# Metaformer block on one core: another order of the two tiles in router, convolution and end, and dummy matmuls in waits

## The chip, the cores and the metric

The kernel runs on one core of a Trainium2 chip. A core has five engines with a program of their own: TensorE (PE, matrix products), VectorE (DVE), ScalarE (ACT), GpSimd (POOL) and SyncE (SP, which here sends for data). They meet through semaphores alone. The metric is the device time of one execution in microseconds, median over the runs. The profile shows for TensorE the clock that was granted: 1.00 is 2.4 GHz, 0.50 is 1.2 GHz.

## The reference

The input `x` is (8, 32, 24, 24) in float32. Four residual parts follow each other; each normalises over the 32 channels of a pixel first:

```python
x = x + neighbour_attention(_ln_c(x))        # 4 heads, 3x3 neighbours, softmax over the nine
t = _to_tokens(x)
t = t + experts(_ln_t(t))                    # 16 experts: softmax of the logits over the 576 tokens,
                                             # the 8 best tokens pooled, gelu layer of 128, result put
                                             # back to those 8 tokens with their probabilities
x = _from_tokens(t, x)
x = x + patch_attention(_ln_c(x))            # 1x1 convolution, 9x9 patches, a @ (b^T @ c) / 9
t = _to_tokens(x)
t = t + steps(_ln_t(t))                      # 33 steps, each: op = argmax(h[0, 0, :19]); attention
                                             # and/or a two-layer relu network, where a mask allows op
```

Of the 33 steps most change nothing, since their masks exclude the chosen operation. With these inputs one step runs, and it is a relu network.

## The kernel before, in words

The eight images are two tiles, t = 0 and 1, of 128 rows each (4 images x 32 channels) and 576 pixels, worked in halves of 288. All of it stays on the chip. Each engine has one program, and the order of the work on an engine is the order of the calls written there (for PE the list of lines 690 to 800); no scheduler stands behind it.

- **Normalisation i of tile t** (i = 0 to 3, ahead of each part): PE subtracts the mean (`centre` L468, or `add_centred` L527 where the terms of a sum are added up centred), ACT squares (L906), DVE keeps the centred values (L1086), PE averages (`variance` L478), ACT forms the inverse deviation (`inverse_std`, L920 and L922), PE widens it to all rows (`widen` L488), DVE multiplies (`scale` L1093, or `patches` L1104 for the convolution).
- **Attention.** Products of q and neighbours on DVE and POOL, `head_sum` L518, softmax on DVE and ACT with the sum of exponentials on PE (L717); `spread` L541 copies the weights over the channels, DVE multiplies by v (L1121), POOL and DVE sum in threes, `add_centred` adds input and sums.
- **Router.** `gate` L549 (logits), ACT adds the bias (L929), DVE `selection` finds the eight best (L1128 to L1131) and forms `pick` (L1134), ACT `probabilities` (L934). PE `turn_y` L557 and `turn_pick` L567 transpose, `pooling` L576, `replicate` L582 and L583, `hidden` L590 and L593, `expert_out` L601, `expert_turn` L608, `scatter_centred` L616 and `scatter_raw` L623 put the results back.
- **Convolution.** `pixels_out` L636, DVE writes the columns (L1177), `mab_product` L646, ACT copies U (L955), `gram_pair` L660, DVE masks (L1185), ACT copies (L961), `values_of` L670, ACT copies (L966), `turn_back` L680, DVE `residual3` adds (L1191).
- **Choice and step.** `token_of` L686 brings the first token to one row, DVE `choose` (L1199 to L1209) finds the operation and reads the number of the next step that has work from a table `code` into `ctrl`. `strike_out` (L1214, L1216) takes the steps up to that one out of the table. Every engine then runs a loop that goes on while `ctrl` names a step: SP sends for its weights (L373 to L377), PE runs L856 and L866, ACT and DVE the relus (L1067, L1366), DVE adds the result to y (L1377). POOL adds y = h + x after the last normalisation (L448), which holds if no step has work.
- **Dummies.** `keep_clock(n, bank)` L461 runs n matmuls of 288 columns whose result nobody reads. Before, it stands around the sum of exponentials alone, two and two.

Of the kernel before, what the change touches and what calls it, by code (L numbers as in the profile page):

```python
# [11 lines left out]
T = B // TB  # L12
# [10 lines left out]
R, NP = 9, 3  # L23
# [130 lines left out]
def metaformer(nc, x, L1_ffn_ffn_w1, L1_ffn_ffn_b1, L1_ffn_ffn_w2, L1_ffn_ffn_b2, L1_ffn_wq, L1_ffn_wk, L1_ffn_wv, L1_ffn_wo,  # L154
# [5 lines left out]
    with ctx:  # L160
# [173 lines left out]
        @block.sync  # L334
        def _(sp):
            for g in range(2):
                sp.dma_start(cut(x_in, 0)[:, g, :], x[0:TB].rearrange("b c h w -> (b c) (h w)")[:, g * HS:(g + 1) * HS]).then_inc(x_ld[g], 16)
            sp.dma_start(mask_w[:, :], masks).then_inc(mask_ld, 16)
            sp.dma_start(rowc[:, :], codes).then_inc(mask_ld, 16)
            sp.dma_start(qkv_bd[:, :, :].rearrange("p a b -> p (a b)"), qkv).then_inc(qkv_ld, 16)  # L340
            sp.dma_start(wpk[:, :], pack).then_inc(pack_ld, 16)
            sp.dma_start(ew1[:, :, :].rearrange("p e h -> p (e h)"), experts1).then_inc(ew1_ld, 16)
            sp.dma_start(ew2[:, :, :].rearrange("p e o -> p (e o)"), experts2).then_inc(ew2_ld, 16)
            for t in range(T):
                sp.dma_start(U[:, t, :, GW:GW + V2], values).then_inc(value_ld, 16)


            steps, cr, row_no = (sp.alloc_register(n) for n in ("sp_steps", "sp_code", "sp_row"))
            sp.reg_mov(steps, 0)
            sp.wait_ge(ctrl_rdy, 1)  # L350
            sp.reg_load(cr, ctrl[0:1, 0:1])
            with sp.While(lambda: sp.snap(cr) < NONE):
                c_ = sp.snap(cr, min_val=0, max_val=NONE - 1)
                sp.reg_mov(row_no, (c_ >> 16) * NOPS + ((c_ >> 1) & 31))
                rw = sp.snap(row_no, min_val=0, max_val=NB_ * NOPS - 1)

                def of_step(w):

                    if len(w.shape) == 4:
                        return w.rearrange("b o c d -> (b o) c d")[bass.ds(rw, 1), :, :].rearrange("o c d -> (o c) d")  # L360
                    return w.rearrange("b o c -> (b o) c")[bass.ds(rw, 1), :].rearrange("o c -> c o")

# [15 lines left out]
                sp.reg_add(steps, steps, 1)  # L378
                wait_for(sp, ctrl_rdy, sp.snap(steps, min_val=1, max_val=NB_) + 1)
                sp.reg_load(cr, ctrl[0:1, 0:1])  # L380

            done = sp.snap(steps, min_val=0, max_val=NB_)
            for t in range(T):
                wait_for(sp, fin_rdy[t], done + 1)
                sp.dma_start(out[t * TB:(t + 1) * TB].rearrange("b c h w -> (b c) (h w)"), y[:, t, :]).then_inc(out_st, 16)
            sp.wait_ge(out_st, 16 * T)
# [3 lines left out]
        def _(pool):  # L390
# [61 lines left out]
        def _(pe):  # L452
# [268 lines left out]
            spread(0)  # L721
            spread(1)
            spread(2)
# [22 lines left out]
            gate(0)  # L746
            turn_y(0)
            variance(1, 1)
            turn_pick(0)
            widen(1, 1)  # L750
            pooling(0)
            gate(1)
            replicate(0)
            turn_y(1)
# [3 lines left out]
            turn_pick(1)  # L758
            expert_out(0)
            pooling(1)  # L760
            expert_turn(0)
            replicate(1)
            scatter_centred(0)
            hidden(1)
            scatter_raw(0)
            expert_out(1)
            variance(2, 0)
            expert_turn(1)
            widen(2, 0)
            scatter_centred(1)  # L770
            scatter_raw(1)
            pixels_out(0)
            variance(2, 1)
            mab_product(0)
            widen(2, 1)
            for k in range(4):
                gram_pair(0, k)
            pixels_out(1)
# [3 lines left out]
            mab_product(1)  # L782
            values_of(0, 2)
            for k in range(4):
                gram_pair(1, k)
            turn_back(0)
            values_of(1, 0)
            pe.wait_ge(x3_rdy[0], 1)
            token_of(xs[3])
            gram_pair(1, 4)  # L790
            centre(3, 0)
            values_of(1, 1)
            variance(3, 0)
            values_of(1, 2)
# [99 lines left out]
        def _(act):  # L894
# [109 lines left out]
            logits(0)  # L1004
            probabilities(0)
            inverse_std(1, 1)
# [42 lines left out]
            with act.While(lambda: act.snap(cr) < NONE):  # L1049
# [10 lines left out]
                with act.If((c_ & 1) > 0):  # L1060
# [9 lines left out]
                    for t in range(T):  # L1070
                        wait_for(act, fin_rdy[t], act.snap(steps, min_val=0, max_val=NB_) + 2)
# [10 lines left out]
        def _(dve):  # L1082
# [42 lines left out]
            def selection(t):  # L1125
# [5 lines left out]
                nc.vector.match_replace(rest[:, t, :], top8[:, t, :], logit[:, t, :], -3e38).then_inc(rest_rdy[t], 1)  # L1131
                dve.wait_ge(rest_rdy[t], 1)
# [87 lines left out]

            keep(0, 0, 0)
# [42 lines left out]
            scale(1, 1)  # L1264
            turned_pick(0)
            pooled_images(0)
            selection(1)
# [23 lines left out]
            residual3(0, 0)  # L1291
            choose(0, 0)
            residual3(0, 1)
            residual3(0, 2)
# [17 lines left out]
            with dve.While(lambda: dve.snap(cr) < NONE):  # L1312
                strike_out(dve.snap(steps, min_val=0, max_val=NB_))
                c_ = dve.snap(cr, min_val=0, max_val=NONE - 1)
                with dve.If((c_ & 256) > 0):
# [34 lines left out]
                    for t in range(T):  # L1350
                        dve.wait_ge(fin_rdy[t], 1)
# [18 lines left out]
                with dve.If((c_ & 1) > 0):  # L1370
# [12 lines left out]
                    for t in range(T):  # L1383
                        dve.wait_ge(fin_rdy[t], 1)
# [11 lines left out]
                dve.sem_inc(step_end, 1)  # L1396
                wait_for(dve, ctrl_rdy, dve.snap(steps, min_val=1, max_val=NB_) + 1)
                dve.reg_load(cr, ctrl[0:1, 0:1])

# [26 lines left out]
```

## Time and profile before

| | |
|---|---|
| time, median of 3 runs | 155.51 us (152.48 to 155.91) |
| the profiled execution | 155.16 us, its span 153.3 us |
| mean granted clock of TensorE | 0.771 |
| busy: PE, DVE, ACT, POOL | 129.2 (84%), 68.0 (44%), 43.5 (28%), 46.7 us (30%) |

Times in the trace count from the start of the span. In the page's second section each digit is a tenth of busy time in one of 40 slices of 3.8 us, and the line PEclk is the granted clock in tenths. The chain that ended last is followed back from the last instruction: each row starts when it was released, and lasts until it released the next. A count behind a matmul row counts passes; a float32 matmul is two of them, a transposition one.

### The profile page before, as it was taken

What the parts mean: (1) busy time and instruction counts of PE and PEld (TensorE: products, weight loads), DVE (VectorE), ACT (ScalarE), POOL (GpSimd) and SP (SyncE); (2) the same over time, 40 slices, a digit from 0 to 9 for tenths busy, and PEclk for the clock granted to TensorE, in tenths of its full rate; (3) what the DMA queues carried; (4) which work ended last, traced back from release to release, by engine and by line L of the source; (5) the groups of instructions that cost most, each with busy time, mean ns of one, the idle gap of its engine ahead of it and who ended that gap; (6) DMA issues with size and microseconds to landing.
All of it is one profiled execution on the core that took longest, in us unless ns stands there. A gap on an engine that the chain in (4) does not pass through costs nothing.

```text
span 153.3 us, 2162 instructions
## 1 busy us (share of the span) xinstructions
PE 129.2 (84%) x779; PEld 86.5 (56%) x779; DVE 68.0 (44%) x148; ACT 43.5 (28%) x104; POOL 46.7 (30%) x37
## 2 busy tenths in 40 slices
PE   0998989959999996669699999999999969647980
PEld 0365548923445572656599685775985836514630
DVE  0246985477645616232410312532650542445860
ACT  3251430410000506602810052114326314132622
POOL 8994950007917899930000000000000000303000
PEclk9999999996559999655555555559999965995567
DMA  5980000000000000000000000000000000010004
GB/s 155 377 181 0 4 0 4 0 0 0 2 0 0 0 4 0 2 0 0 0 0 0 4 0 0 0 0 0 0 0 4 0 0 0 4 17 4 2 4 154
DMA packets 3394, 3.55 MB, mean 23 GB/s; under 512 B 1974, under 2 KB 2614, under 8 KB 3384
## 3 DMA queue, kind: packets, MB, share of 16 engines
q1 hardware_dynamic: 3096, 2.90, 6.3%
q10 hardware_dynamic: 288, 0.51, 0.9%
q8 instruction: 7, 0.11, 0.3%
q14 instruction: 3, 0.02, 0.1%
HBM read 2.81 MB, written 0.59 MB: 22 GB/s over the span
## 4 chain that ended last, share of the span: by engine, by line
PE 78%; DVE 8%; ACT 6%; issue 4%; DMA 2%; DVEq 1%; ACTq 0%
PE PS L527 9%; PE PS L541 7%; PE PS L494 5%; PE PS L468 5%; PE PS L488 4%; PE PS L856 4%; PE PS L660 4%; PE PS L670 4%; PE PS L636 4%; PE PS L576 4%; PE PS L646 3%; PE PS L567 3%; PE PS L623 3%; PE PS L616 3%; PE PS L518 3%
## 5 line engine op out<-in xcount | busy, mean ns | idle before, releaser
L448 POOL TENSOR_TENSOR y<-h,x 128x576 f32<-128x576 f32 x2 | 2.8, 1406 | 70.1 <-DVE h L1093 70.1
L1121 DVE TENSOR_TENSOR prods<-PS,vpad 128x432 f32<-128x432 f32 x24 | 13.2, 601 | 6.2 <-PE PS L541 5.9
L906 ACT ACTIVATE sq<-PS 128x288 f32<-128x288 f32 x12 | 4.9, 412 | 32.8 <-PE PS L527 22.2
L423 POOL TENSOR_TENSOR prods<-prods 128x576 f32<-128x576 f32 x6 | 8.4, 1404 | 19.0 <-DVE prods L1121 18.7
L541 PE MATMUL PS<-attn,wpk 32*128 32x432 f32 x48 | 11.7, 751 | 1.8 <-DVE prods L1121 1.4
L527 PE MATMUL PS<-prods,cst 128*128 128x288 f32 x36 | 12.3, 480 | 0.0
L527 PEld LDWEIGHTS PS<-prods,cst 128*128 128x128 f32 x36 | 7.3, 219 | 6.2 <-issue 3.3
L1086 DVE COPY xc<-PS 128x288 f32<-128x288 f32 x10 | 4.6, 457 | 11.8 <-ACT sq L906 11.8
L488 PE MATMUL PS<-rstd,cst 64*128 64x144 f32 x64 | 7.6, 365 | 1.3 <-ACT rstd L922 1.3
L494 PE MATMUL PS<-y,qkv_bd 128*128 128x288 f32 x24 | 7.4, 431 | 1.4 <-DVE y L1093 1.0
L413 POOL TENSOR_TENSOR prods<-q_sb,kpad 128x576 f32<-128x576 f32 x6 | 7.7, 1318 | 2.1 <-ACT q_sb L983 2.1
L1110 DVE TENSOR_TENSOR prods<-PS,kpad 128x576 f32<-128x576 f32 x12 | 8.1, 744 | 0.0
L488 PEld LDWEIGHTS PS<-rstd,cst 64*128 64x128 f32 x64 | 5.7, 234 | 3.8 <-ACT rstd L922 2.1
L541 PEld LDWEIGHTS PS<-attn,wpk 32*128 32x128 f32 x48 | 3.7, 235 | 7.4 <-issue 4.0
L856 PE MATMUL PS<-h,fw 32*128 32x384 f32 (+1 forms) x32 | 6.4, 730 | 1.7 <-issue 1.7
L468 PE MATMUL PS<-x_in,cst 128*128 128x288 f32 x8 | 4.0, 619 | 4.0 <-DMA cst<-in_first 4.0
L660 PE MATMUL PS<-U,xT 65*117 65x181 f32 x40 | 7.1, 324 | 0.1
L1093 DVE TENSOR_TENSOR y<-PS,xc 128x288 f32<-128x288 f32 x8 | 3.3, 451 | 8.6 <-PE PS L488 8.6
L576 PE MATMUL PS<-pickT,yT 96*128 96x64 f32 x24 | 5.6, 423 | 1.5 <-DVE pickT L1139 1.5
L1185 DVE TENSOR_TENSOR gram<-PS,wpk 117x234 f32<-117x234 f32 x10 | 3.9, 398 | 6.3 <-PE PS L660 6.2
L670 PE MATMUL PS<-gram,cval 117*64 117x117 f32 x40 | 6.5, 311 | 0.0
L660 PEld LDWEIGHTS PS<-U,xT 65*117 65x117 f32 x40 | 6.0, 180 | 0.7 <-issue 0.6
(128 smaller groups left out, 235.0 us busy)
## 6 DMA issues: line engine op xcount, KB each, us to landing
wpk<-in_pack SPq DMA_DIRECT2D x1, 849.0 KB, 5.5
result<-y SPq DMA_DIRECT2D x2, 288.0 KB, 2.2
ew<-in_experts SPq DMA_DIRECT2D x2, 256.0 KB, 6.2
U<-in_values SPq DMA_DIRECT2D x2, 162.5 KB
x_in<-in_x SPq DMA_DIRECT2D x2, 144.0 KB, 3.5
x_in<-in_x ACTq DMA_DIRECT2D x1, 288.0 KB, 4.2
cst<-in_first ACTq DMA_DIRECT2D x1, 209.0 KB, 3.2
qkv_bd<-in_qkv SPq DMA_DIRECT2D x1, 192.0 KB, 3.5
```

What stands on the lines that cost most here:

```text
L423: nc.gpsimd.tensor_tensor(total, a, prods[:, t, m * TRI + 1, :], ALU.add).then_inc(gsum_rdy[t], 1)
L468: nc.tensor.matmul(PS[:, AB[t][g], 0:HS], con("cen"), cut(src, t)[:, g, :], start=True, stop=True).then_inc(xc_done[t], 1)
L488: last = nc.tensor.matmul(PS[:, AB[t][g], par * QS:(par + 1) * QS], sel[64 * g:64 * g + 64, par, :], rstd[64 * g:64 * g + 64, t, :], start ...
L494: nc.tensor.matmul(PS[:, bank, 0:HS], qkv_bd[:, w, :], cut(y, t)[:, g, :], start=True, stop=True).then_inc(signal, 1)
L527: done = nc.tensor.matmul(PS[:, AB[t][g], 0:HS], con("cen"), term[:, g * HS:(g + 1) * HS], start=first, stop=last, skip_group_check=True)
L541: nc.tensor.matmul(PS[:, 4 + q, 0:TRI * QS], heads[32 * q:32 * q + 32, t, :], attn[32 * q:32 * q + 32, m * TRI:(m + 1) * TRI, :].rearrange ...
L576: last = nc.tensor.matmul(PS[:, CD[t][1], 0:ER], yT[:, t, c, :], pickT[:, t, c, :], start=(c == 0), stop=(c == NCH - 1))
L660: last = nc.tensor.matmul(PS[0:GW, BK[t][GRAM_BANK[k]], i * (GW + V2):(i + 1) * (GW + V2)], xT[:, t, g * GW:(g + 1) * GW], U[:, t, g, :], ...
L670: last = nc.tensor.matmul(PS[0:V2, BK[t][YV_BANK[k]], i * GW:(i + 1) * GW], cval[:, t, 4 * k + i, :], gram[:, t, 4 * k + i, :], start=True ...
L856: nc.tensor.matmul(PS[:, BK[t][j], 0:F1W[k]], fw1[j * C:(j + 1) * C, :], h[j * C:(j + 1) * C, t, w], start=True, stop=True).then_inc(f1_do ...
L1110: nc.vector.tensor_tensor(prods[:, t, n, :].rearrange("p (g r c) -> p g r c", g=2, c=WW), rows24(both(AB[t])), k, ALU.mult).then_inc(prod_ ...
L1121: nc.vector.tensor_tensor(prods[:, t, m * TRI:(m + 1) * TRI, q * QS:(q + 1) * QS].rearrange("p n (r c) -> p n r c", c=WW), PS[:, 4 + q, 0: ...
```

## The change

1. *Softmax.* The adds of the two input tiles go from ahead of the sum of exponentials to behind `spread(0)` and `spread(1)`; the dummies ahead of the sum become four.
2. *Router.* Normalisation 1 of the second tile (`variance(1,1)`, `widen(1,1)`; ACT `inverse_std(1,1)`; DVE `scale(1,1)`) goes ahead of the first tile's `turn_pick` and `picked`, which is split from `selection`. Both tiles' router steps alternate in another order, with nine calls of `keep_clock`, twelve dummies in all. `widen(2,0)` goes behind both scatters of the second tile, `variance(2,1)` ahead of `pixels_out(0)`.
3. *Convolution.* `pixels_out(1)` goes ahead of `gram_pair(0,*)`, `mab_product(1)` ahead of `values_of(0,0)`, `values_of(0,2)` behind `gram_pair(1,*)`.
4. *End.* All three residuals of the first tile stand ahead of the choice; the first `strike_out` between `scale(3,0)` and the second tile's residuals, the later ones at the loop's end instead of its start. `widen(3,0)` goes behind `turn_back(1)`; four calls of `keep_clock`, seven dummies, stand around `variance(3,1)` and `widen(3,1)`; PE reads `ctrl` ahead of `variance(3,1)`.
5. *Step.* DVE raises `step_end` once at the start, so that SP sends for weights as soon as the choice is made. POOL's two adds go; DVE does them where no step has work.

The core of the diff:

```diff
@@ PE
-            add_centred(0, x_in[:, 0, :], first=True)
-            add_centred(1, x_in[:, 1, :], first=True)
             pe.wait_ge(mab_rdy, 1)
-            keep_clock(2, VBANK)
+            keep_clock(4, VBANK)
...
             spread(0)
+            add_centred(0, x_in[:, 0, :], first=True)
             spread(1)
+            add_centred(1, x_in[:, 1, :], first=True)
             spread(2)
...
             widen(3, 0)
-            turn_back(1)
+            keep_clock(1, 6)
             centre(3, 1)
-            variance(3, 1)
-            widen(3, 1)
-
+            keep_clock(2, 6)
             cr = pe.alloc_register("pe_code")
             pe.wait_ge(ctrl_rdy, 1)
             pe.reg_load(cr, ctrl[0:1, 0:1])
+            variance(3, 1)
+            keep_clock(2, 6)
+            widen(3, 1)
+            keep_clock(2, 6)
@@ DVE
+            dve.sem_inc(step_end, 1)
             keep(0, 0, 0)
...
             selection(0)
             scale(1, 1)
+            picked(0)
+            selection(1)
             turned_pick(0)
             pooled_images(0)
-            selection(1)
+            picked(1)
...
-            residual3(0, 0)
+            for i in range(NP):
+                residual3(0, i)
             choose(0, 0)
-            residual3(0, 1)
-            residual3(0, 2)
             gram_mask(1, 4)
             keep(3, 0, 0)
             keep(3, 0, 1)
             scale(3, 0)
+            strike_out(0)
             for i in range(NP):
                 residual3(1, i)
-            dve.sem_inc(step_end, 1)
...
             with dve.While(lambda: dve.snap(cr) < NONE):
-                strike_out(dve.snap(steps, min_val=0, max_val=NB_))
...
                 dve.sem_inc(step_end, 1)
+                strike_out(dve.snap(steps, min_val=1, max_val=NB_))
@@ POOL
-            for t in range(T):
-                pool.wait_ge(h_rdy[t], 2)
-                pool.wait_ge(x3_rdy[t], NP)
-                nc.gpsimd.tensor_tensor(y[:, t, :], h[:, t, :], xs[3][:, t, :], ALU.add).then_inc(fin_rdy[t], 1)
```

The order that this gives is shown at three places. PE in the router, from the first tile's `gate` on, before (lines are those of each kernel's own text):

```order
L549 MATMUL PS<-y,wpk 64x288 x2
L557 MATMUL PS<-wpk,y 96x128 x6
L478 MATMUL PS<-sq,cst 32x144 x4
L567 MATMUL PS<-diag,pick 96x64 x6
L488 MATMUL PS<-rstd,cst 128x144 x4
L576 MATMUL PS<-pickT,yT 128x64 x6
L549 MATMUL PS<-y,wpk 64x288 x2
L582 MATMUL PS<-pooled_j,wpk 128x64
L583 MATMUL PS<-wpk 128x64
L557 MATMUL PS<-wpk,y 96x128 x6
L590 MATMUL PS<-pooled_e,ew 128x16 x4
L593 MATMUL PS<-wpk 128x64
```

And now (`gate` is L546, `variance` L475, `turn_y` L554, `widen` L485, the dummies L458, `turn_pick` L564, `pooling` L573):

```order
L546 MATMUL PS<-y,wpk 64x288 x2
L475 MATMUL PS<-sq,cst 32x144 x4
L554 MATMUL PS<-wpk,y 96x128 x6
L485 MATMUL PS<-rstd,cst 128x144 x4
L458 MATMUL PS<-x_in,cst 128x288 x2
L546 MATMUL PS<-y,wpk 64x288 x2
L458 MATMUL PS<-x_in,cst 128x288 x3
L564 MATMUL PS<-diag,pick 96x64 x6
L458 MATMUL PS<-x_in,cst 128x288
L554 MATMUL PS<-wpk,y 96x128 x6
L573 MATMUL PS<-pickT,yT 128x64 x6
L458 MATMUL PS<-x_in,cst 128x288
```

The second tile's `variance`, `widen` and `gate` moved ahead of the first tile's `turn_pick`, and its `turn_y` ahead of the first tile's `pooling`.

PE in the convolution, from the first `gram_pair` (L660 before) to the second tile's, before:

```order
L488 MATMUL PS<-rstd,cst 128x144 x4
L660 MATMUL PS<-U,xT 117x181 x8
L636 MATMUL PS<-wpk,y 64x130 x9
L670 MATMUL PS<-gram,cval 64x117 x4
L660 MATMUL PS<-U,xT 117x181 x2
L670 MATMUL PS<-gram,cval 64x117 x4
L646 MATMUL PS<-xT,mab 65x390 x3
L670 MATMUL PS<-gram,cval 64x117 x2
L660 MATMUL PS<-U,xT 117x181 x8
```

And now (`gram_pair` L657, `pixels_out` L633, `mab_product` L643, `values_of` L667):

```order
L485 MATMUL PS<-rstd,cst 128x144 x4
L643 MATMUL PS<-xT,mab 65x390 x3
L633 MATMUL PS<-wpk,y 64x130 x9
L657 MATMUL PS<-U,xT 117x181 x8
L643 MATMUL PS<-xT,mab 65x390 x3
L667 MATMUL PS<-gram,cval 64x117 x4
L657 MATMUL PS<-U,xT 117x181 x2
L667 MATMUL PS<-gram,cval 64x117 x4
L657 MATMUL PS<-U,xT 117x181 x8
```

`pixels_out` of the second tile left the place between gram matrices and values, and `mab_product` took it.

DVE at the end, from the last of `choose` (L1208, L1209) to the loop, before (`residual3` L1191, gram mask L1185, centred values L1086, `scale` L1093):

```order
L1208 TENSOR_REDUCE ctrl<-code 1x1
L1209 TENSOR_REDUCE nextf<-code 1x1
L1191 TENSOR_TENSOR x<-PS,x 128x3x8x8 x2
L1185 TENSOR_TENSOR gram<-PS,wpk 117x234
L1086 COPY xc<-PS 128x288 x2
L1093 TENSOR_TENSOR h<-PS,xc 128x288 x2
L1191 TENSOR_TENSOR x<-PS,x 128x3x8x8 x3
L1086 COPY xc<-PS 128x288 x2
L1093 TENSOR_TENSOR h<-PS,xc 128x288 x2
L1310 TENSOR_LOAD ctrl
```

And now (`residual3` L1203, `scale` L1102, `strike_out` L1226 and L1228):

```order
L1220 TENSOR_REDUCE ctrl<-code 1x1
L1221 TENSOR_REDUCE nextf<-code 1x1
L1197 TENSOR_TENSOR gram<-PS,wpk 117x234
L1095 COPY xc<-PS 128x288 x2
L1102 TENSOR_TENSOR h<-PS,xc 128x288 x2
L1226 TENSOR_SCALAR late<-wpk,nextf 1x33
L1228 TENSOR_TENSOR code<-code,late 1x627
L1203 TENSOR_TENSOR x<-PS,x 128x3x8x8 x3
L1095 COPY xc<-PS 128x288 x2
L1102 TENSOR_TENSOR h<-PS,xc 128x288 x2
L1324 TENSOR_LOAD ctrl
```

`strike_out` stands between `scale(3,0)` and the second tile's residuals, which it followed before, in the loop.

## Rows read from the trace of the kernel before

**Rows 1.** The page: granted clock in tenths, shares of the chain.
```profile
PEclk9999999996559999655555555559999965995567
...
PE 78%; DVE 8%; ACT 6%; issue 4%; DMA 2%; DVEq 1%; ACTq 0%
```

**Rows 2.** Stretches: length, busy (instructions) of PE, PEld, DVE, ACT, POOL, clock, DMA, GB/s
```profile
35.30:45.60 10.30, 10.30 (x29) 4.37 (x28) 5.92 (x12) 0.00 (x0) 7.01 (x5) 0.50 0.00 1
...
57.80:62.60 4.80, 2.08 (x20) 0.98 (x20) 3.36 (x7) 3.31 (x9) 4.64 (x4) 1.00 0.00 0
62.60:79.70 17.10, 14.26 (x69) 12.01 (x69) 4.02 (x10) 6.13 (x15) 3.83 (x3) 0.50 0.00 0
79.70:101.20 21.50, 21.05 (x80) 16.03 (x80) 6.05 (x17) 3.87 (x8) 0.00 (x0) 0.50 0.00 1
...
124.10:130.90 6.80, 6.29 (x30) 4.22 (x32) 1.68 (x5) 2.61 (x7) 0.00 (x0) 0.50 0.00 0
```

**Rows 3.** Chain of waits, router: start, length, engine, line, passes.
```profile
57.83 0.69 PE PS L549 x4
...
62.52 2.04 PE PS L567 x12
...
67.16 2.79 PE PS L576 x12
69.95 1.21 PE PS L549 x4
...
75.16 1.86 PE PS L590 x8
...
96.02 1.34 PE PS L488 x8
...
101.18 3.34 PE PS L636 x18
```

**Rows 4.** Chain of waits, dummies and the neighbour attention.
```profile
27.60 0.97 PE PS L461 x4
...
34.51 5.76 PE PS L541 x16
40.27 2.22 PE PS L527 x4
42.49 1.75 PE PS L541 x8
44.24 1.85 PE PS L527 x4
...
48.18 1.03 PE PS L541 x8
49.21 1.17 PE PS L527 x4
```

**Rows 5.** Timeline, attention: start, length, engine, line, operation, shapes, count.
```profile
33.24 3.39 DVE L1121 TENSOR_TENSOR prods<-PS,vpad 128x432 f32<-128x432 f32 x6
```

**Rows 6.** Chain of waits, convolution, second tile's pixels and gram matrices.
```profile
110.41 2.14 PE PS L636 x18
...
117.92 2.69 PE PS L660 x16
```

**Rows 7.** Timeline, VectorE, convolution, second tile's columns.
```profile
111.26 1.89 DVE L1177 TENSOR_TENSOR xT<-PS,wpk 64x390 f32<-64x390 f32 x3 [0.41 <-PE PS L636]
```

**Rows 8.** Timeline, VectorE in the router, POOL and VectorE at the step.
```profile
72.98 0.14 DVE L1130 TENSOR_SCALAR ntop<-top 64x1 f32<-64x1 f32 x1
...
138.12 1.40 POOL L448 TENSOR_TENSOR y<-h,x 128x576 f32<-128x576 f32 x1 [4.42 <-DVE h L1093]
138.34 1.22 DVE L1214 TENSOR_SCALAR late<-wpk,nextf 1x33 f32<-1x33 f32 x1 [0.29 <-issue]
...
139.71 0.80 DVE L1216 TENSOR_TENSOR code<-code,late 1x627 f32<-1x627 f32 x1 [0.15 <-DVE late L1214]
```

**Rows 9.** Chain of waits, PE ahead of the first layer.
```profile
137.13 1.71 issue
```

More of the change, by code:

```diff
@@ L345, in _ @@
                 sp.dma_start(U[:, t, :, GW:GW + V2], values).then_inc(value_ld, 16)
-            steps, cr, row_no = (sp.alloc_register(n) for n in ("sp_steps", "sp_code", "sp_row"))
+            steps, cr, row_no, need = (sp.alloc_register(n) for n in ("sp_steps", "sp_code", "sp_row", "sp_need"))
             sp.reg_mov(steps, 0)
+            sp.reg_mov(need, 1)
             sp.wait_ge(ctrl_rdy, 1)
@@ L378, in _ @@
                 sp.reg_add(steps, steps, 1)
+                sp.reg_mov(need, sp.snap(steps, min_val=1, max_val=NB_))
                 wait_for(sp, ctrl_rdy, sp.snap(steps, min_val=1, max_val=NB_) + 1)
                 sp.reg_load(cr, ctrl[0:1, 0:1])
-            done = sp.snap(steps, min_val=0, max_val=NB_)
+            results = sp.snap(need, min_val=1, max_val=NB_)
             for t in range(T):
-                wait_for(sp, fin_rdy[t], done + 1)
+                wait_for(sp, fin_rdy[t], results)
                 sp.dma_start(out[t * TB:(t + 1) * TB].rearrange("b c h w -> (b c) (h w)"), y[:, t, :]).then_inc(out_st, 16)
@@ L746, in _ @@
             gate(0)
+            variance(1, 1)
             turn_y(0)
-            variance(1, 1)
+            widen(1, 1)
+            keep_clock(2, 7)
+            gate(1)
+            keep_clock(3, 7)
             turn_pick(0)
-            widen(1, 1)
+            keep_clock(1, 7)
+            turn_y(1)
             pooling(0)
-            gate(1)
+            keep_clock(1, 7)
             replicate(0)
-            turn_y(1)
+            turn_pick(1)
             pe.wait_ge(ew1_ld, 16)
@@ L757, in _ @@
             hidden(0)
-            turn_pick(1)
+            keep_clock(1, 7)
+            pooling(1)
             expert_out(0)
-            pooling(1)
+            keep_clock(1, 0)
+            replicate(1)
             expert_turn(0)
-            replicate(1)
+            hidden(1)
+            keep_clock(1, 0)
             scatter_centred(0)
-            hidden(1)
+            expert_out(1)
             scatter_raw(0)
-            expert_out(1)
+            keep_clock(1, 2)
+            expert_turn(1)
             variance(2, 0)
-            expert_turn(1)
-            widen(2, 0)
+            keep_clock(1, 2)
             scatter_centred(1)
             scatter_raw(1)
+            widen(2, 0)
+            variance(2, 1)
             pixels_out(0)
-            variance(2, 1)
+            widen(2, 1)
             mab_product(0)
-            widen(2, 1)
+            pixels_out(1)
             for k in range(4):
                 gram_pair(0, k)
-            pixels_out(1)
+            mab_product(1)
             values_of(0, 0)
@@ L781, in _ @@
             values_of(0, 1)
-            mab_product(1)
-            values_of(0, 2)
             for k in range(4):
                 gram_pair(1, k)
+            values_of(0, 2)
             turn_back(0)
             values_of(1, 0)
+            gram_pair(1, 4)
             pe.wait_ge(x3_rdy[0], 1)
             token_of(xs[3])
-            gram_pair(1, 4)
             centre(3, 0)
             values_of(1, 1)
+            values_of(1, 2)
             variance(3, 0)
-            values_of(1, 2)
+            turn_back(1)
             widen(3, 0)
-            turn_back(1)
+            keep_clock(1, 6)
             centre(3, 1)
-            variance(3, 1)
-            widen(3, 1)
+            keep_clock(2, 6)
             cr = pe.alloc_register("pe_code")
@@ L1004, in _ @@
             logits(0)
+            inverse_std(1, 1)
             probabilities(0)
-            inverse_std(1, 1)
             turned_y(0)
@@ L1070, in _ @@
                     for t in range(T):
-                        wait_for(act, fin_rdy[t], act.snap(steps, min_val=0, max_val=NB_) + 2)
+                        wait_for(act, fin_rdy[t], act.snap(steps, min_val=0, max_val=NB_) + 1)
                         for k in range(2):
@@ L1131, in selection, with picked @@
                 nc.vector.match_replace(rest[:, t, :], top8[:, t, :], logit[:, t, :], -3e38).then_inc(rest_rdy[t], 1)
+            def picked(t):
                 dve.wait_ge(rest_rdy[t], 1)
@@ L1349, in _ @@
                         nc.vector.tensor_copy(h0[:, bass.ds(b, 1), :].rearrange("c b (g s) -> c (b g) s", g=2), PS[0:C, 6:8, 0:HS]).then_inc(at_dve, 1)
-                    for t in range(T):
-                        dve.wait_ge(fin_rdy[t], 1)
                     wait_for(dve, at_dve, na * ADVE_R + ADVE_R)
@@ L1382, in _ @@
                     wait_for(dve, fw2_ld, nf * 48 + 48)
-                    for t in range(T):
-                        dve.wait_ge(fin_rdy[t], 1)
                     choose(dve.snap(steps, min_val=1, max_val=NB_), 448, lambda k: result(0, k))
@@ L1396, in _ @@
                 dve.sem_inc(step_end, 1)
+                strike_out(dve.snap(steps, min_val=1, max_val=NB_))
                 wait_for(dve, ctrl_rdy, dve.snap(steps, min_val=1, max_val=NB_) + 1)
                 dve.reg_load(cr, ctrl[0:1, 0:1])
+            with dve.If(dve.snap(steps, min_val=0, max_val=NB_) < 1):
+                for t in range(T):
+                    dve.wait_ge(h_rdy[t], 2)
+                    nc.vector.tensor_tensor(y[:, t, :], h[:, t, :], xs[3][:, t, :], ALU.add).then_inc(fin_rdy[t], 1)
 def kernel(**inputs):
```

## The prediction, made before the result was known

> **What bounds the kernel now.** I read the page first. Its chain of the work that ended last is TensorE for most of the span, and its clock line shows that engine at about half speed in several stretches [rows 1]. So the two questions of this change are what stands on TensorE's path, and at which of its two levels (1.2 and 2.4 GHz) it is worked off. The table of stretches answers the second [rows 2]. From 35.3 to 45.6 us the clock is 0.50 and PE is busy all the time; from 57.8 to 62.6 it is 1.00 but PE is busy for 2.08 of 4.80 us, waiting while the logits become `pick`; then it is 0.50 to 101.2, with PE busy 14.26 of 17.10 and then 21.05 of 21.50 us. The last two rows matter most: in the router the clock stayed low through 38 us in which PE hardly paused. The chain of waits gives the price: `gate` takes 0.69 us at the high level and 1.21 at the low, a ratio of 0.57 [rows 3]. What the change must buy with its dummies is therefore large. A dummy unit is one matmul of 288 columns; two of them take 0.97 us [rows 4], so 0.48 each at the high level and, estimated by the halved level, up to 0.96 at the low.
>
> **The sum, part by part**, in the frame of the profiled execution: span 153.3, time 155.16 us, so 1.86 lie around the span; it ran 0.35 under the median of 155.51.
>
> *Softmax.* The two first adds of the input leave the stretch ahead of the sum of exponentials, where two dummies of the same shape take their place (nothing changes there), and go behind `spread(0)` and `spread(1)`. There PE now waits for VectorE's products, 3.39 for six, 0.565 each [rows 5], and after that wait the clock falls. I take it that the filled wait keeps the clock. Then the pieces at the low level shrink to what the same pieces take later at the high one [rows 4]: 2.22 and 1.85 to 1.17, 1.75 to 1.03, together 2.45. The first piece of 5.76 can't go below its eight products, 8 x 0.565 = 4.5: another 1.2. **-3.6**; the ends are 0 (the clock falls all the same) and -4.0. `gate(0)` then starts at 54.2 instead of 57.83.
>
> *Router up to `hidden(0)`.* With 54.2 as zero, at the high level: after `gate(0)` VectorE is through with the first tile's `selection` at 3.4 (as before, 57.83 to 61.26), but `scale(1,1)` of 0.82 now stands there, so `picked(0)` ends at 5.3. PE meanwhile can start `gate(1)` only behind that scale, 4.5 to 5.2, and the three dummies behind it, 1.4, hold `turn_pick(0)` to 6.65, 1.2 later than `pick` is there. Then, durations at the low level [rows 3] times 0.57: `turn_pick(0)` 1.2, a dummy and `turn_y(1)` 1.4, `pooling(0)` 1.6, a dummy 0.5, `replicate(0)` 0.7, `turn_pick(1)` 1.2, `hidden(0)` 1.4. That is 14.6, so 68.7 on the clock of the span. Before, the same work was done at 79.7: 11 us, of which 3.6 are the softmax's. This is the gain the change is made of.
>
> *Router from there.* I take it that the clock then falls. The groups that follow are those beside which it stayed low for 38 us while PE hardly paused [rows 2], and five single dummies among them are 2.4 us more of work in 20. At the low level the rest is the 21.4 us of before (79.74 to 101.18), less `widen(2,0)` 1.34 and the wait of 0.8 ahead of it, and `expert_turn(1)` of 0.4, which now counts: 19.7. Five dummies add 4.8. `hidden(1)` now stands right behind `expert_turn(0)`, and VectorE must write the expert blocks (0.60) and the pooled rows (0.23) in between: 1.1 with the hand-overs. `widen(2,0)`, 1.34, now comes after both scatters; behind it VectorE writes the patches (1.15) and adds the experts (0.9), ScalarE squares (0.44), and only then `variance(2,1)` runs: 2.9 of waiting, and the variance itself 0.7, which no longer stands behind `pixels_out(0)` (0.4 back). Sum 68.7 + 19.7 + 4.8 + 1.1 + 1.3 + 2.9 + 0.7 - 0.4 = 98.8, against 101.18 [rows 3]: of the 11 us **-2.4** are left. The ends are the rivals' below.
>
> *Convolution.* `pixels_out(1)` goes ahead of the first tile's gram matrices, `mab_product(1)` ahead of `values_of(0,0)`. From the end of `gram_pair(0,*)` to the start of `gram_pair(1,*)` there were 117.92 - 110.41 = 7.51, of which `pixels_out(1)` 2.14: 5.37 [rows 6]. Now VectorE first finishes four gram masks (0.7 past the end), then writes the columns, 1.89 for three [rows 7], the first at 1.3; `mab_product(1)` 2.14 ends at 3.4; two values groups and a gram pair, 2.56, at 6.0; and ScalarE copies U for the second tile only behind the copy of `values_of(0,1)`, 0.6 and three of 0.49: 8.0. **+2.6.** Behind it `values_of(0,2)` stands alone before `turn_back(0)` (1.2 with its copy), while the residuals no longer wait for the choice: +0.4.
>
> *End.* `widen(3,0)` moves behind `turn_back(1)`, and on VectorE `scale(3,0)`, 0.82, and `strike_out(0)` stand before `residual3(1,*)`. `strike_out` took 1.22 and 0.80 [rows 8], but the first of these, 33 numbers, ran beside POOL's add of 1.40, which started 0.22 earlier; alone, such an instruction takes 0.14 elsewhere [rows 8]. POOL's add is gone, so I take 0.14 + 0.15 + 0.80 = 1.1; if the row were the instruction's own length it would be 2.2. The Trainium skill ("SBUF — State Buffer", section "Who interferes with whom") has the rule that fits the short value: a tensor_scalar of VectorE in its two-port mode and GpSimd exclude each other for a whole instruction. The trace agrees with it in that one pair (1.22 beside POOL, 0.14 without). Until the second tile's residuals start, from `values_of(1,1)` on, the path was 5.2 us; it is now 1.75 + 0.97 + 0.64 + 0.7 + 1.1 + 0.1 + 0.82 + 1.1 = 7.1: **+1.9**. The dummies around `variance(3,1)` and `widen(3,1)` lie in waits for ScalarE and VectorE of 0.85 to 1.1: +0.3 at the high level, 2 at the low. One more stretch at the low level between 101 and the layers, like that of 124.1 to 130.9 [rows 2], costs 6.8 x 0.43 = 2.9 and 1.4 for its dummies; the old pauses are gone but two new ones (in the convolution and before the residuals) stand there, so I take half: **+2.1**.
>
> *Step and tail.* PE's read of the control word moves ahead, out of the 1.71 between `widen(3,1)` and the first layer [rows 9]: -0.5. `strike_out` leaves the start of the loop on VectorE (138.34 to 140.51), so its share of the relus starts earlier, and with dummies before it the layer runs partly at the high level: -2.5 (ends 0 and -4). At the loop's end `strike_out` stands after VectorE's last wait, and that engine is already the last to come to its end: +1.1. The weights sent for at the choice: 0, their transfers land at 136.8 and before, the layer starts at 138.84 and waits for `h`. POOL's adds: 0, their results are overwritten by the step. **-1.9.**
>
> Sum: -2.4 + 2.6 + 0.4 + 1.9 + 0.3 + 2.1 - 1.9 = **+3.0**: span 156.3, time 158.2, and 158.5 against the median.
>
> **The rivals.** *The clock holds in the router* (faster). Speaks for it: the longest wait, 57.8 to 62.6, is filled with the second tile's normalisation and five dummies, and PE is given hardly a pause from then on. Then the rest costs 19.7 x 0.57 + 5 x 0.48 and the same waits, 68.7 + 11.2 + 2.4 + 1.1 + 0.8 + 2.9 = 87.1, and `pixels_out(0)` 2.14 for 3.34: -15.3. With the convolution and the end as above but without the low stretch (+5.2), that stretch's 2.9 gained and the tail, the time is 155.5 - 15 = 140.5; where it holds for half of the way, 148. It decides at the end of `hidden(0)`. Against it: 21.05 busy of 21.50 us at 0.50 [rows 2]. The Trainium skill ("TensorE: Matmul & The Clock Gate", Part 1) says that sustained activity brings the high level and idling the low; by it alone a PE that hardly pauses would hold its clock, and this rival would be the likeliest. The row of 21.50 us shows a busy PE that stayed low, so I give it 0.24.
>
> *The clock falls at the old place or sooner* (slower): in the softmax all the same, or between `gate(0)` and `pooling(0)`. Each dummy then costs up to 0.96 on the path: five or six ahead of `pooling(0)` and at most 2 us of matmuls more, +5; without the softmax's gain, +3.6. 162 to 167. Chance 0.2.
>
> *Gain and price cancel*: the clock falls some 4 us later than I take it, or the end's low stretch doesn't come. 151 to 155.5. Chance 0.17.
>
> *The change doesn't do part of what it says*: the early request for weights brings nothing, as said above; this is in the sum.
>
> **How the numbers follow.** My forecast, 155.5 to 161.5, has 0.39. The likeliest is 158.5. About 2% (3.1 us, 152.4 to 158.6) is what a measurement of this kernel tells from no change, as its three runs spread over 3.4. Faster: 0.24 and a little of the cancelling case, 0.26. Slower: the second rival, 0.2, and just over half of the forecast, 0.42. Within: the rest, 0.32. The range, 146 to 164, leaves out the better half of the first rival and the worse part of the second.
>
> **What would show it.** In the changed profile: the clock at 1.00 from 8 to past 60 us (softmax right); `gate(0)` near 54; `hidden(0)` ended near 69 and the clock low from about there (router right; high there, the first rival); a pause of PE of 2 us ahead of the second tile's gram matrices and ScalarE's U copies as what ends it; VectorE's `late` at about 0.15; VectorE as the engine that ends last. I am wrong above all if the row of `pixels_out(0)` starts before 92 or after 103.

## The result, and the profile after

The changed kernel takes 163.8 us (median of 4 runs, 163.32 to 164.04) against 155.08 (152.48 to 155.91): 1.066 times the kernel before, with a 95% interval of 1.0525 to 1.08. The profiled execution took 164.04, its span is 162.2 us, 8.9 more than before. I had forecast 158.5, slower by 3.0. The direction and the range held; the size was off by nearly a factor of three. Executions of one kernel can fall into a faster and a slower group: the ratios below compare the faster groups, plain times are medians of all executions, and the traces of a, c, e and m are of slower ones.

The page of the changed kernel, sections 2 and 4, as [rows 1]:

```profile
PEclk9999999999999999975555555998555557959996
...
PE 78%; DVE 8%; ACT 6%; issue 3%; DMA 2%; DVEq 1%; ACTq 0%
```

The mean granted clock rose from 0.771 to 0.814 and the kernel got slower. The low stretch of the attention is gone, that of the router is shorter, and a new one stands where the convolution had run at full clock. The table of stretches, as [rows 2] (length, then busy time and instructions of PE, PEld, DVE, ACT, POOL, then clock, DMA share, GB/s):

```profile
54.80:71.00 16.20, 15.64 (x117) 11.95 (x116) 8.89 (x18) 9.47 (x24) 8.58 (x6) 1.00 0.01 3
71.00:101.70 30.70, 27.73 (x101) 19.72 (x100) 7.14 (x19) 4.61 (x10) 0.00 (x0) 0.50 0.00 0
101.70:112.00 10.30, 9.25 (x54) 6.29 (x53) 4.72 (x11) 2.52 (x7) 0.00 (x0) 1.00 0.01 2
112.00:135.80 23.80, 21.47 (x80) 16.47 (x79) 4.95 (x16) 5.27 (x16) 0.00 (x0) 0.50 0.00 0
135.80:142.70 6.90, 3.49 (x33) 2.33 (x32) 2.82 (x7) 1.30 (x4) 0.00 (x0) 0.99 0.08 14
142.70:146.10 3.40, 3.40 (x15) 1.70 (x13) 0.91 (x2) 0.82 (x2) 0.00 (x0) 0.50 0.00 0
146.10:159.70 13.60, 9.46 (x88) 5.55 (x84) 7.52 (x21) 5.73 (x14) 0.00 (x0) 1.00 0.10 38
```

The fourth row is the loss: 23.8 us at 1.2 GHz. Just before it PE is busy for 9.25 of 10.30 us at full clock, with one pause in it. The timeline of PE shows that pause and the next (in brackets the idle time ahead, and what ended it):

```profile
110.65 2.90 PE L643 MATMUL PS<-xT,mab 65*65 65x390 f32 x6 [1.05 <-DVE xT L1189]
...
120.42 5.15 PE L657 MATMUL PS<-U,xT 65*117 65x181 f32 x16 [1.88 <-ACT U L964]
```

The clock fell at 111.96, 1.3 us after the first pause. The second row is `gram_pair(1,*)`, 5.15 us for what took 2.69 before [rows 6]. The chain through it, as [rows 6]:

```profile
106.95 2.67 PE PS L657 x16
109.64 0.40 DVE gram L1197
110.04 0.47 DVE xT L1189
110.51 0.14 issue
110.65 2.90 PE PS L643 x6
113.55 1.75 PE PS L667 x8
115.30 1.49 PE PS L657 x4
116.79 1.77 PE PS L667 x8
118.58 0.56 ACT prods L975
119.14 1.15 ACT U L964 x3
120.29 0.14 issue
120.42 5.15 PE PS L657 x16
```

It reads as forecast: gram masks, then columns, then `mab_product`, values, and ScalarE's copies of U behind the copy of the values. Only the lengths differ, since from the middle of `mab_product(1)` on everything is at the low level: 10.8 us from the end of `gram_pair(0,*)` to the start of `gram_pair(1,*)`, where 8.0 were forecast.

One way to see where the 8.9 us came from is to cut the span where a stage begins (starts of the first matmuls in the timelines of the two profiled executions):

| | before | after | difference | forecast |
|---|---|---|---|---|
| to `gate(0)` | 57.8 | 54.8 | -2.9 | -3.6 |
| `gate(0)` to `pixels_out(0)` | 43.35 | 43.1 | -0.3 | +1.2 |
| `pixels_out(0)` to `turn_back(0)` | 19.4 | 29.1 | +9.6 | about +3 |
| `turn_back(0)` to the end | 32.7 | 35.2 | +2.5 | about +2.4 |

### The profile page after: what moved, and what is told of

It is laid out like the page before. It is cut to its first block, busy times and chain, and to the rows that moved or that the text cites. A ratio compares the mean times of both kernels' runs of the same rounds, so it can differ in the third digit from the quotient of the medians.

```text
span 162.2 us, 2247 instructions
## 1 busy us (share of the span) xinstructions
PE 138.3 (85%) x821; PEld 91.8 (57%) x821; DVE 68.4 (42%) x150; ACT 42.3 (26%) x104; POOL 43.9 (27%) x35
## 4 chain that ended last, share of the span: by engine, by line
PE 78%; DVE 8%; ACT 6%; issue 3%; DMA 2%; DVEq 1%; ACTq 0%
PE PS L458 9%; PE PS L524 7%; PE PS L657 7%; PE PS L538 5%; PE PS L667 5%; PE PS L465 5%; PE PS L491 5%; PE PS L633 4%; PE PS L485 3%; PE PS L643 3%; PE PS L613 3%; PE PS L475 3%; PE PS L620 3%; PE PS L598 2%; PE PS L865 2%
## 5 line engine op out<-in xcount | busy, mean ns | idle before, releaser
L458 PE MATMUL PS<-x_in,cst 128*128 128x288 f32 x50 | 19.2, 504 | 0.0
L915 ACT ACTIVATE sq<-PS 128x288 f32<-128x288 f32 x12 | 4.9, 412 | 31.6 <-PE PS L524 19.0
L657 PE MATMUL PS<-U,xT 65*117 65x181 f32 x40 | 11.0, 444 | 1.9 <-ACT U L964 1.9
L458 PEld LDWEIGHTS PS<-x_in,cst 128*128 128x128 f32 x50 | 9.8, 221 | 4.5 <-issue 2.3
L657 PEld LDWEIGHTS PS<-U,xT 65*117 65x117 f32 x40 | 9.3, 260 | 3.0 <-issue 3.0
L524 PE MATMUL PS<-prods,cst 128*128 128x288 f32 x36 | 10.6, 426 | 0.0
L538 PE MATMUL PS<-attn,wpk 32*128 32x432 f32 x48 | 9.2, 572 | 0.6 <-DVE attn L1266 0.4
L667 PE MATMUL PS<-gram,cval 117*64 117x117 f32 x40 | 8.9, 403 | 0.0
L667 PEld LDWEIGHTS PS<-gram,cval 117*64 117x64 f32 x40 | 7.3, 223 | 2.9 <-issue 2.0
L465 PE MATMUL PS<-x_in,cst 128*128 128x288 f32 x8 | 4.6, 728 | 3.9 <-DMA cst<-in_first 3.9
L475 PE MATMUL PS<-sq,cst 128*32 128x144 f32 x64 | 5.3, 372 | 2.3 <-ACT sq L915 2.1
L975 ACT COPY prods<-PS 64x468 f32<-64x468 f32 (+1 forms) x6 | 2.9, 491 | 16.0 <-PE PS L667 16.0
L485 PE MATMUL PS<-rstd,cst 64*128 64x144 f32 x64 | 6.7, 327 | 0.3 <-ACT rstd L931 0.3
L485 PEld LDWEIGHTS PS<-rstd,cst 64*128 64x128 f32 x64 | 5.2, 203 | 3.0 <-issue 2.0
```

The lines of the kernel that those rows point to most:

```text
L458: nc.tensor.matmul(PS[:, bank, 0:HS], con("cen"), cut(x_in, 0)[:, 0, :], start=True, stop=True)
L465: nc.tensor.matmul(PS[:, AB[t][g], 0:HS], con("cen"), cut(src, t)[:, g, :], start=True, stop=True).then_inc(xc_done[t], 1)
L475: last = nc.tensor.matmul(PS[32 * q:32 * q + 32, AB[t][0], 0:QS], con("mean"), sq[:, t, q * QS:(q + 1) * QS], start=True, stop=True)
L485: last = nc.tensor.matmul(PS[:, AB[t][g], par * QS:(par + 1) * QS], sel[64 * g:64 * g + 64, par, :], rstd[64 * g:64 * g + 64, t, :], start ...
L524: done = nc.tensor.matmul(PS[:, AB[t][g], 0:HS], con("cen"), term[:, g * HS:(g + 1) * HS], start=first, stop=last, skip_group_check=True)
L538: nc.tensor.matmul(PS[:, 4 + q, 0:TRI * QS], heads[32 * q:32 * q + 32, t, :], attn[32 * q:32 * q + 32, m * TRI:(m + 1) * TRI, :].rearrange ...
```

## The experiments

Two theories. PAUSE: the loss is the clock, which falls because PE waits in the new order of the convolution. WORK: the loss is the added dummies and waits themselves. A third, ORDER, came up with the first runs: the clock falls because of which matmuls stand there, waiting or not. For the two kernels and all twelve runs the same three stages, from each one's profiled execution (the fall is that of the router, counted from `gate(0)`; the end is that of the span):

| kernel | time, us | fall after `gate(0)` | `gate(0)` to `pixels_out(0)` | to `turn_back(0)` | to the end |
|---|---|---|---|---|---|
| before | 154.6 to 155.5 | 4.9 | 43.35 | 19.4 | 32.7 |
| after | 163.8 | 16.2 | 43.1 | 29.1 | 35.2 |
| a_softmax | 151.4 | 6.4 | 42.0 | 20.7 | 32.5 |
| b_no_router_dummies | 163.1 | 8.4 | 43.2 | 29.1 | 34.7 |
| c_conv_old | 154.5 | 15.0 | 44.1 | 24.2 | 31.6 |
| d_end_old | 164.4 | 16.4 | 42.9 | 28.95 | 35.8 |
| e_conv_fill | 157.5 | 13.2 | 45.6 | 23.8 | 31.6 |
| f_u_first | 162.9 | 15.2 | 41.2 | 26.0 | 35.3 |
| i_conv_old_no_late | 150.9 | 13.2 | 40.8 | 21.7 | 31.5 |
| j_router_conv_old | 151.2 | 6.4 | 42.0 | 20.7 | 31.5 |
| m_waits_gone | 153.7 | 13.1 | 45.8 | 20.5 | 31.5 |
| k_strike_first | 149.2 | 15.9 | 38.5 | 20.7 | 33.4 |
| l_strike_both | 147.1 | 16.3 | 38.1 | 21.15 | 30.6 |
| n_no_end_dummies | 146.7 | 15.4 | 39.0 | 20.3 | 31.4 |

### c_conv_old: PE's old order of the convolution

```diff
-            pixels_out(1)
             for k in range(4):
                 gram_pair(0, k)
-            mab_product(1)
+            pixels_out(1)
             values_of(0, 0)
             gram_pair(0, 4)
             values_of(0, 1)
+            mab_product(1)
+            values_of(0, 2)
             for k in range(4):
                 gram_pair(1, k)
-            values_of(0, 2)
```

> The change with PE's order of the convolution as before (pixels_out(1) behind gram_pair(0,*), mab_product(1) behind values_of(0,1), values_of(0,2) ahead of gram_pair(1,*)). Theory PAUSE: the two waits of 1.05 and 1.88 us ahead of mab_product(1) and gram_pair(1,*) go, the clock does not fall at 112, and the 24 us at 0.50 shrink to less than 8: 155 to 158 us. Theory WORK: only the 2.6 us of the order itself come back: 161 to 161.5.

154.5 us, 0.988 of the kernel before (0.980 to 0.996): 9.3 less than the change, for three moved calls. WORK's 161 is out. The stretches of this kernel from 102.9 us on:

```profile
102.90:106.30 3.40, 2.73 (x12) 1.13 (x11) 1.16 (x3) 1.46 (x3) 0.00 (x0) 1.00 0.00 0
106.30:113.20 6.90, 6.90 (x28) 6.48 (x27) 2.16 (x5) 1.06 (x4) 0.00 (x0) 0.51 0.01 2
113.20:130.20 17.00, 15.60 (x117) 11.65 (x115) 5.96 (x18) 7.44 (x19) 0.00 (x0) 1.00 0.01 3
```

The clock still fell once, at 106.3, behind another wait of PE (0.67, for U of the first tile), but it came back at 113.2 and PE ran the rest of the convolution at full clock.

A wait does not decide alone, however. The same wait of 0.67 stands at full clock in i, k, l and n, whose order of the convolution is c's. The first row is c's, the second k's:

```profile
105.98 4.82 PE L657 MATMUL PS<-U,xT 65*117 65x181 f32 x16 [0.67 <-ACT U L964]
...
101.09 2.69 PE L657 MATMUL PS<-U,xT 65*117 65x181 f32 x16 [0.67 <-ACT U L959]
```

Behind it the clock was low for 6.8 us in c and for 3.4 in i and l, and in k and n it held for more than 20 us. What makes the difference no run shows.

### m_waits_gone and e_conv_fill: the new order without its pauses

m moves no matmul. It makes early what PE waits for:

```diff
@@ DVE
+            pixels(1)
             for k in range(4):
                 gram_mask(0, k)
-            pixels(1)
@@ ACT
+            for k in range(NP):
+                u_copy(1, k)
             yv_copy(0, 0)
             cval_copy(0, 4)
             yv_copy(0, 1)
-            for k in range(NP):
-                u_copy(1, k)
```

> The change with PE's order untouched and no dummy added, but with what PE waits for in the convolution made earlier: VectorE writes the second tile's columns ahead of the first tile's gram masks, ScalarE copies U of the second tile ahead of the first tile's values. Theory PAUSE: neither wait is there, the clock does not fall at 112 or only for a short stretch, 155 to 158.5 us, as with the waits filled by dummies (157.5). Rival ORDER: the clock falls at 112 all the same, the waits alone come back, 161 to 162.

153.7 us (148.56 to 154.59), 10 less than the change. The timeline of PE in the same place shows the two rows without a wait ahead of them, and at full clock:

```profile
112.70 2.16 PE L643 MATMUL PS<-xT,mab 65*65 65x390 f32 x6
...
117.49 2.72 PE L657 MATMUL PS<-U,xT 65*117 65x181 f32 x16
```

e leaves the waits and fills them:

```diff
+            keep_clock(2, 3)
             mab_product(1)
             values_of(0, 0)
             gram_pair(0, 4)
             values_of(0, 1)
+            keep_clock(4, 2)
             for k in range(4):
                 gram_pair(1, k)
```

> The change with two more dummies ahead of mab_product(1) and four ahead of gram_pair(1,*), in the two pauses of PE of 1.05 and 1.88 us; order unchanged. Theory PAUSE (the clock falls at 112 because PE waits there): it stays at 1.00 through the convolution or falls for one short stretch; two or three of the units lie in the waits, the others cost 0.5 each: 155 to 158 us. Rival ORDER (the clock falls at 112 because of which matmuls stand there, pause or not): it falls all the same, and the six units cost up to 3 more: 164 to 167.

157.5 us (152.2 to 157.93): six matmuls more, 6.3 us less, and no execution of e or m came near the change's 163.3 to 164.0. The clock was 1.00 in this stretch:

```profile
105.80:124.40 18.60, 18.16 (x102) 13.05 (x98) 6.17 (x15) 5.37 (x15) 0.00 (x0) 1.00 0.00 1
```

PE's order is that of the change in both, so ORDER falls with WORK. What was late brought the clock down. m's stage takes 20.5 against 29.1 us; the two waits themselves are 2.9 of these 8.6, so by subtraction about 5.6 are the clock's. e's stage, 23.8, is m's and the 3.35 of its six dummies.

### f_u_first: the second wait alone

The ACT half of m.

> The change with ScalarE's three copies of U for the second tile ahead of its copies of values_of(0,0) and values_of(0,1), so that gram_pair(1,*) need not wait for them; the pause of 1.05 ahead of mab_product(1) stays. If the first pause alone brings the clock down: it falls at 112 as before, only the wait of 1.9 goes, and 161.5 to 162.5 us are left. If the second one counts as well, the clock comes back some 3 to 10 us earlier than 135.85: 157 to 160.

162.9 us (158.27 to 164.87); the trace is that of the execution of 158.27. There the clock fell at 106.65, right behind the first wait:

```profile
106.02 3.55 PE L643 MATMUL PS<-xT,mab 65*65 65x390 f32 x6 [1.05 <-DVE xT L1189]
```

It came back at 130.54, 23.9 us later as in the change, although the second wait is gone. The first pause alone is enough. The stage got 3.1 shorter: 1.9 are the second wait, and `pixels_out(0)` ran at full clock (2.21 instead of 4.04), while `mab_product(1)` took 0.65 longer. The 158.27 lies in the range of the other expectation, but not by its reason: the clock came back in this execution's router at 89.6 already, 20.5 us after its fall, where the change has 30.7. No run shows why.

### b_no_router_dummies and i_conv_old_no_late: what the router's dummies are worth

b takes all twelve away, i (with c's order of the convolution) the five behind `hidden(0)`.

```diff
             widen(1, 1)
-            keep_clock(2, 7)
             gate(1)
-            keep_clock(3, 7)
             turn_pick(0)
...
             hidden(0)
-            keep_clock(1, 7)
             pooling(1)
```

> The change without its twelve dummies in the router, all else as in the change. Theory PAUSE (the loss is a clock that falls in new pauses of PE and costs what the dummies won): the clock falls some 8 us earlier, at 62 to 64 instead of 71, the work up to hidden(0) gets 3 us longer for its matmuls and 3.4 shorter for its dummies, the five late ones give back 5: pixels_out(0) starts at 92 to 94 instead of 98, and the convolution's low stretch stays: 158 to 160 us. Theory WORK (the loss is the added matmuls on PE's path): 12 units of 0.5 to 1.3 us go, 9 to 10 in all: 154 to 155.

> The change with PE's old order of the convolution and without the five dummies of the router behind hidden(0), which ran at 0.50 and took 0.96 to 1.26 us each on PE's path. If they hold no clock: 5 to 6 us less than with them (154.5): 148.5 to 150 us. If they are what brings the clock back to 1.00 at 102 to 103: it comes 3 to 7 us later and eats 2 to 3 of it, 151 to 152.5.

b: 163.1 us, and neither expectation was near, though the clock fell at 62.5, where PAUSE had put it; `pixels_out(0)` started at 97.3 instead of 92 to 94. i: 150.9, between its two expectations, 0.978 of the kernel before (0.971 to 0.984), 3.6 less than c. Its clock came back 30.7 us after the fall, as in the change, so the late dummies did not bring it back. The stage from `gate(0)` explains both, read at an equal instant of the clock's fall, which differs by up to 3.3 us between kernels whose code is the same up to there. With the five late dummies the stage takes 45.6 and 45.8 where the clock falls 13.1 to 13.2 after `gate(0)` (e, m) and 43.1 where it falls at 16.2 (after); without them 40.8 at 13.2 (i) and 38.1 at 16.3 (l). The difference is 4.9 to 5.0 in both pairs, 0.98 a dummy: at the low level they are plain work. (f, whose clock came back early, is not comparable here.) The seven early ones keep the clock until 13 to 16 us where it falls at 8.4 without them (b): 43.2 against the 38.1 to 39.0 of k, l and n and the 40.8 of i, so they win 2.4 to 5.1 net of their cost, more the later the clock falls. In the change the late ones give back what the early ones win, and b saw no difference of note (163.1 against 163.8).

### d_end_old and n_no_end_dummies

d undoes the end's dummies and its order, n (on i) the dummies alone.

```diff
             widen(3, 0)
-            keep_clock(1, 6)
             centre(3, 1)
-            keep_clock(2, 6)
...
             variance(3, 1)
-            keep_clock(2, 6)
             widen(3, 1)
-            keep_clock(2, 6)
```

> The change with the end as before: none of the seven dummies, widen(3,0) ahead of turn_back(1), the first strike_out behind scale(3,1) and not between scale(3,0) and the second tile's residuals. Theory PAUSE: 2.0 us of order come back and the two dummies at the low level, 1.9: 159.5 to 160.5, unless the clock, with no dummies, stays low until the step: then the layers take 2 us more, 162. Theory WORK: seven units and the order, 6 us: 157.5 to 158.5.

> The change with the old order of the convolution and without the late router dummies (150.9), and without the seven dummies of the end; its order of the end stays. If they hold the clock for the two layers (1.00 from 133 to 147 with them): it falls before or in the layers, which then take 2 to 3 us more, and 1 to 1.5 come back ahead of them: 152 to 153. If they only cost: 149 to 150.

d: 164.4 us, nothing gained, and above all that was expected. Its last stage takes 35.8 against 35.2, with the clock fallen again ahead of the step's first layer (146.28) and low into it; its stretches there:

```profile
139.60:149.90 10.30, 8.31 (x40) 4.84 (x40) 3.25 (x9) 3.18 (x8) 0.00 (x0) 0.50 0.01 1
149.90:153.30 3.40, 2.69 (x21) 1.67 (x24) 3.40 (x8) 1.81 (x5) 0.00 (x0) 1.00 0.00 0
```

n: 146.7 us, 4.2 less than i, but that is not the dummies: the last stages are 31.4 and 31.5 long, and the 4.2 stand ahead of them, where the two kernels have the same code (the router's fall at 15.4 instead of 13.2, and one short low stretch less in the convolution). Without the dummies n comes from the second tile's residuals to the first layer in 7.3 us (i 8.3) and takes 13.9 from there to the end (i 13.0), with the clock at 0.50 until 134.48, the first 3.4 us of the layer. So the end's seven dummies cost about 1 and win about 1; d, which changes the order as well, can't tell the two apart.

### a_softmax and j_router_conv_old: the parts that pay

a is the kernel before with the softmax part, j the change with router and convolution as before.

```diff
             spread(0)
+            add_centred(0, x_in[:, 0, :], first=True)
             spread(1)
+            add_centred(1, x_in[:, 1, :], first=True)
             spread(2)
```

> The kernel before with the softmax part of the change alone (first adds behind the spreads, four dummies). Both theories say the same here, it sizes the term: if the filled wait keeps the clock at 1.00 past 35 us, the attention shrinks by 3.6 us and gate(0) starts at 54.2 to 54.9 instead of 57.8; 151 to 152.5 us. If the clock falls at 35 all the same: 155.

> The change with router and convolution as before, on PE, VectorE and ScalarE, and no dummies there: softmax, end and step of the change alone. Softmax alone gave 151.4. If end and step are worth what the tail showed (2 us from h to the end) and their order costs 2 to 3 ahead of it: 150.5 to 152 us, and the router's new order (154.5 with the old convolution) costs 3. If the end's order and dummies cost at any clock: 154.

a: 151.4 us, 0.973 (0.964 to 0.981). j: 151.2, 0.982 (0.974 to 0.990). The softmax part is worth about 3 us, a little under the 3.6 of the forecast: `gate(0)` begins at 55.2 in a, 2.5 earlier than before, where 2.9 to 3.6 were expected. With the new end and step the last stage is 31.5 (j) and not 32.5 (a), but the times of a and j do not tell the two apart. j, with the old router, also sizes the new one: c, with all twelve dummies, is 3.3 us slower than j, i without the five late ones is level with it, and k, l and n, where the clock falls later and the end differs a little, are 2 to 4.5 faster.

### k_strike_first and l_strike_both: a version that beats both

On i, the first `strike_out` behind `scale(3,1)` (k), and in l the loop's one ahead of the last wait for `h`.

```diff
             scale(3, 0)
-            strike_out(0)
             for i in range(NP):
                 residual3(1, i)
...
             scale(3, 1)
+            strike_out(0)
@@ in the loop (l alone)
+                strike_out(dve.snap(steps, min_val=1, max_val=NB_))
                 for t in range(T):
...
                 dve.sem_inc(step_end, 1)
-                strike_out(dve.snap(steps, min_val=1, max_val=NB_))
```

> The change with the old order of the convolution and without the late router dummies (150.9), and with the first strike_out behind scale(3,1) instead of ahead of the second tile's residuals. Both strike_out instructions stood on the path there for 1.0 us, and behind scale(3,1) VectorE waits for the layer's first matmuls anyway: 149.7 to 150.1 us. If they only filled a wait there, or if the relus start later by them: 150.7 to 151.2.

> As the one before, and in the loop strike_out stands ahead of the last wait for h instead of behind it, where it delayed VectorE, the engine that ends last, by 1.0 us. If VectorE sets the end: another 0.8 to 1.0 less, 148.7 to 149.3. If the results' transfers set it: no change against the one before.

k: 149.2 us, 0.962 (0.947 to 0.976). l: 147.1, 0.956 (0.946 to 0.967), 8 us faster than the kernel before and 17 faster than the change. For k's own move the times prove nothing: its last stage is 33.4, longer than i's, with the clock low from 121.71 to 128.54 and again from 138.78 to 142.19, and its router took 2.3 less than i's with the same code. l's last stage is 30.6, the shortest of all, 0.9 below i's. Whether that is the loop's move or the clock's place, these runs do not separate. n, with neither move, is as fast (146.7).

## Why the prediction was wrong in size

**The step that failed** is the one that priced the low clock behind the router: "One more stretch at the low level between 101 and the layers, like that of 124.1 to 130.9 [rows 2], costs 6.8 x 0.43 = 2.9 and 1.4 for its dummies; the old pauses are gone but two new ones (in the convolution and before the residuals) stand there, so I take half: +2.1". I had found the pauses, the engines that make them and nearly their length, and then summed the convolution at the high level, 8.0, and added half a short stretch. Measured: 23.9 us at 0.50, and 29.1 instead of 19.4 us from `pixels_out(0)` to `turn_back(0)`, where the sum had about 3 more. c, e and m show that the pauses brought this on, and not the order or the work: with what PE waits for made early (m) the stage takes 20.5. Why the clock stayed low for 24 us, and not for the 6.8 that I had taken from the kernel before, stays open.

**The router** went as forecast, in place and in reason. `gate(0)` at 54.9 (54.2), `hidden(0)` ended at 69.1 (68.7), the clock fell at 71.0 (69), `pixels_out(0)` at 98.0 (98.8). The rows, as [rows 3]:

```profile
54.91 0.69 PE PS L546 x4
...
67.74 0.99 PE PS L587 x8
...
98.00 3.97 PE PS L633 x18
```

The five late dummies were put at 4.8 and cost 4.9. The sign by which I would have been wrong above all, `pixels_out(0)` before 92 or after 103, did not come: it watched the router, and the error lay behind it. The rival in which the clock holds there is out: 27.73 busy of 30.70 us at 0.50. The rule of the Trainium skill that this rival leaned on ("TensorE: Matmul & The Clock Gate", Part 1: sustained activity brings the high level) does not decide here, as before: PE was busy for nine tenths of that stretch.

**The second rival** named a time of 162 to 167 us, and the time lies in it, but by a mechanism that did not occur: softmax and early router kept their clock.

**The end** was put at about +2.4 with half a low stretch in it, and the stage measures +2.5. Here the parts fit too. The chain, before (`values_of(1,1)`, the second tile's residuals, first layer) and now:

```profile
126.90 1.75 PE PS L670 x8
...
132.13 1.06 DVE x L1191 x3
...
138.84 6.42 PE PS L856 x30
```

```profile
133.80 2.36 PE PS L667 x12
...
140.89 1.07 DVE x L1203 x3
...
149.26 0.98 PE PS L865 x8
```

To the residuals it took 5.2 us and takes 7.1, as forecast (6.5 in m, at full clock). From the first layer to the end it took 14.4 and takes 13.0, 1.4 less, also as forecast (-2.5 and +1.1). Between the two, 6.7 became 8.4, with the clock at 0.50 from 142.7 to 146.1; in l, at full clock and with the same dummies, this part takes 6.6. So the half stretch was about enough for this stage; what the sum lacked is the low clock in the convolution.

**strike_out** came out as taken. Without POOL's add its first instruction takes 0.22, and 0.23 at the loop's end:

```profile
139.80 0.22 DVE L1226 TENSOR_SCALAR late<-wpk,nextf 1x33 f32<-1x33 f32 x1
140.06 0.80 DVE L1228 TENSOR_TENSOR code<-code,late 1x627 f32<-1x627 f32 x1
```

It took 1.22 in [rows 8], beside POOL: the long value was a wait for POOL, as the rule of the Trainium skill ("SBUF — State Buffer", "Who interferes with whom") has it.

## What to carry to other kernels

A wait of PE in a stretch at full clock is not priced by its length. One of 1.05 us was followed by 23.9 us at half clock in each of the four traces that have it (the change, b, d, f), and the clock's part of the loss (about 5.6 us) was nearly twice the two waits together; one of 0.67 was followed by nothing, 3.4 or 6.8 us. So where a reordering makes PE wait for the first time, find what is late and make it early (m: two blocks moved on VectorE and ScalarE, 10 us) before adding dummies. Dummies pay where they bridge a wait at full clock (seven in the router won 2.4 to 5.1 us), and are plain work at the low level (0.98 us each). Compare kernels by stage and by the instant at which the clock falls: two with the same code in the router differed by 2.7 us there.

## What was not expected of the hardware

In all eleven traces with the new router order the first tile's `pick` on VectorE takes 1.86 to 1.89 us, where it took 0.82 before. The timeline of the changed kernel:

```profile
58.93 3.28 POOL L437 TENSOR_TENSOR x<-x,prods 128x576 f32<-128x576 f32 x2
59.06 1.88 DVE L1146 SCALAR_TENSOR_TENSOR pick<-rest,prob 64x576 f32<-64x576 f32 x1
...
65.65 0.74 DVE L1146 SCALAR_TENSOR_TENSOR pick<-rest,prob 64x576 f32<-64x576 f32 x1
```

POOL's sum began 0.13 ahead of it, and `pick` lasts one POOL instruction (1.40) less that head start and most of its own 0.74 more; the second tile's, with POOL idle, takes 0.74. In the kernel before, `pick` began 0.29 ahead of POOL's sum. By the Trainium skill ("SBUF — State Buffer", "Who interferes with whom") a VectorE instruction with two inputs in SBUF shares a read port with GpSimd, and whoever issues first holds the other off; the rows agree. The three dummies behind `gate(1)` hide the wait. Without them (b) `turn_pick(0)` waited 1.17 us for `pick`.
